# Additions two visits behind in all three edge passes, and the visits' scalars turned in one transposition

## The reference

```
# layer 0, first attention ("gat", 4 heads)
alpha = segment_softmax(leaky_relu(a_src[src] + a_dst[dst]), dst)
x1    = segment_sum(h[src] * alpha, dst)
# layer 0, second attention ("attn", 1 head)
logits2 = (q[dst] * k[src]).sum(-1) * scale
out     = segment_sum(v[src] * segment_softmax(logits2, dst), dst)
# layer 1 ("typed", 8 heads, edge types and edge weights)
a   = exp(alpha - max[dst]);  a = a / denom[dst] * edge_weight
out = segment_sum(x_src[src] * a, dst)
```

## Time and profile before

| | us |
|---|---|
| median of 3 runs | 5183.95 (5179.76 to 5184.89) |
| the profiled execution | 5139.55 |
| its span, first to last instruction | 5137.6 |
| gat: first to last addition | 217.9 to 1597.0 |
| attn: first to last addition | 1838.8 to 3118.0 |
| typed: first to last addition | 3356.8 to 4745.1 |

### The profile page before, as it was taken

How to read it: one execution, slowest core, us unless ns; L and a number is a source line. 1 busy time by engine, 2 the same in 40 slices (tenths; PEclk the granted TensorE clock), 3 DMA queues, 4 the chain that set the end, 5 groups by cost and what they waited for, 6 DMA issues and landing times. The chain is left out here.

```text
span 5137.6 us, 80902 instructions
## 1 busy us (share of the span) xinstructions
PE 3442.0 (67%) x15488; PEld 2347.2 (46%) x15488; DVE 3184.0 (62%) x11098; ACT 1745.4 (34%) x5660; POOL 2637.8 (51%) x2962
## 2 busy tenths in 40 slices
PE   5366666666666556777777778556666666666899
PEld 4244434444444434444444445334443343444898
DVE  6355555555557655665666667655666666667786
ACT  2323323323334534544554555311111111211333
POOL 3555555555540255555555553555555455552787
PEclk8666666666778878888888898766666666767999
DMA  8444444344432433333333334533333333332321
GB/s 131 137 123 116 119 123 118 113 119 124 120 109 69 134 95 102 110 103 101 104 103 100 104 100 143 183 101 102 108 108 105 103 107 107 106 103 63 90 72 54
DMA packets 289304, 556.41 MB, mean 108 GB/s; under 512 B 86392, under 2 KB 183713, under 8 KB 288898
## 3 DMA queue, kind: packets, MB, share of 16 engines
q0 software_dynamic: 115872, 326.30, 23.3%
q10 hardware_dynamic: 97688, 162.20, 10.4%
q1 hardware_dynamic: 75338, 63.47, 4.8%
HBM read 474.96 MB, written 76.78 MB: 107 GB/s over the span
## 5 line engine op out<-in xcount | busy, mean ns | idle before, releaser
L477 PE MATMUL psum<-big,onehots_or_distances 128*128 128x264 f32 (+2 forms) x4992 | 2186.2, 552 | 940.5 <-DVE big L639 309.6
L661 DVE TENSOR_TENSOR acc<-acc,psum 128x264 f32 (+2 forms) x2496 | 1062.4, 426 | 1071.8 <-PE psum L477 347.3
L477 PEld LDWEIGHTS psum<-big,onehots_or_distances 128*128 128x128 f32 x4992 | 1053.0, 256 | 1296.5 <-issue 1018.3
L266 POOL DMA_INDIRECT big<-table_attn,src_by_edge x782 | 739.8, 946 | 785.2 <-SPq L259 374.2
L266 POOL DMA_INDIRECT big<-table_typed,src_by_edge x782 | 740.1, 946 | 669.6 <-SPq L259 441.5
L266 POOL DMA_INDIRECT big<-table_gat,src_by_edge x782 | 739.1, 945 | 662.6 <-SPq L259 438.5
L370 ACT ACTIVATE onehots_or_distances<-psum 128x512 f32<-128x512 f32 x416 | 248.3, 597 | 1786.9 <-PE psum L437 756.5
L639 DVE TENSOR_TENSOR big<-big,psum 128x256 f32<-128x256 f32 x1664 | 670.2, 408 | 63.0 <-issue 33.7
L423 PE MATMUL psum<-big,onehot_t 128*128 x2496 | 485.9, 309 | 192.2 <-issue 117.7
L343 ACT ACTIVATE onehots_or_distances<-iota,tables 128x128 f32<-128x128 f32 x832 | 331.4, 398 | 679.7 <-DVE acc L661 377.0
L504 DVE SCALAR_TENSOR_TENSOR dot_products<-psum,big 128x258 f32<-128x258 f32 x832 | 347.4, 418 | 319.9 <-PE psum L423 150.6
(11 more groups left out here) (280 smaller groups left out, 4420.6 us busy)
## 6 DMA issues: line engine op xcount, KB each, us to landing
onehot_t<-onehots ACTq DMA_DIRECT2D x68, 512.0 KB
big<-visit_positions ACTq DMA_DIRECT2D x52, 512.0 KB
onehots<-big ACTq DMA_DIRECT2D x36, 512.0 KB
big<-onehots ACTq DMA_DIRECT2D x36, 512.0 KB
big<-in_x_dram SPq DMA_DIRECT2D x98, 128.0 KB, 2.5
big<-table_gat,src_by_edge POOLq DMA_INDIRECT x782
big<-table_attn,src_by_edge POOLq DMA_INDIRECT x782
big<-table_typed,src_by_edge POOLq DMA_INDIRECT x782
```

The costliest lines, as they stand in the source:

```text
L266: pool.indirect_dma_start(X[:, t % RING, :], None, ph.table, bass.IndirectOffsetOnAxis(ap=m.src[:, t:t + 1], axis=0)).then_inc(S[f"rows{t ...
L477: nc.tensor.matmul(sum_ps(v), onehot_at(v), rows, start=True, stop=True).then_inc(S["summed"], 1)
L661: nc.vector.tensor_tensor(row, row, sum_ps(v), ALU.add).then_inc(S["added"], 1)
```

## The change

1. In all passes the DVE loop runs one visit longer and calls `add(v - 2)` at `v` where it called `add(v - 1)`. Loading the block numbers and `rescale` move from `v % 16 == 0` to `v % 16 == 1`. Nothing else in a pass moves: scaling, dot products, the parts of the maximum, PE's, ACT's, SP's and POOL's programs and all semaphore values are as before.
2. The per-chunk store of the scalars (7 DMAs, L898) is gone. DVE writes the three numbers of a chunk to columns of one tile; after the last chunk PE transposes that tile once (`turn_scalars`), ACT copies it out of PSUM and SP stores it with one DMA of contiguous rows, then reads it back as before.

```diff
-            for v in range(-3 * G, VISIT_END + 1):
+            for v in range(-3 * G, VISIT_END + 2):
...
-                if 0 <= v < VISIT_END and v % G == 0:
-                    last_blk, blks = (blks[G - 1] if v else None), blocks_of(v // G)
-                if v >= 1:
-                    add(v - 1, last_blk if v % G == 0 and v < VISIT_END else blks[(v - 1) % G])
+                if 0 <= v < VISIT_END and v % G == 1:
+                    last_blk, blks = (blks[G - 1] if v > 1 else None), blocks_of(v // G)
+                if v >= 2:
+                    add(v - 2, last_blk if v % G == 1 and v < VISIT_END else blks[(v - 2) % G])
...
-                if v >= 0 and v % G == 0 and v < VISIT_END:
+                if v >= 0 and v % G == 1 and v < VISIT_END:
                     rescale(v // G, blks[0])
...
+    scalars, scalar_rows = v_.take(3, VC), v_.take(P)[0:3 * VC]
-    scal = [n_.take(3) for _ in range(2)]
...
+    turned_scalars = ps[0:3 * VC, 6, 2 * P:3 * P]
...
-                sp.dma_start(dram.scal[:, c * P:(c + 1) * P].rearrange("a v -> v a"), scal[c % 2], allow_slow_non_contiguous=True).then_inc(S[f"stored{c % 2}"], 16)
...
+            sp.wait_ge(S["scalar_rows"], 1)
+            sp.dma_start(dram.scal.rearrange("a (c p) -> (a c) p", p=P), scalar_rows).then_inc(S["scalars_stored"], 16)
...
+            act.wait_ge(S["scalars_turned"], 1)
+            nc.scalar.activation(scalar_rows, turned_scalars, ACT.Copy).then_inc(S["scalar_rows"], 1)
...
+            def turn_scalars():
+                pe.wait_ge(S["chunk"], VC)
+                pe.wait_ge(S["packed"], VC - 1)
+                pe.wait_ge(S["packed_rest"], VC - 1)
+                nc.tensor.transpose(turned_scalars, scalars.rearrange("p a c -> p (a c)"), m.ident[:, :]).then_inc(S["scalars_turned"], 1)
...
-                nc.vector.tensor_copy(scal[p][:, 0:2], dst_f[:, 0:P:P - 1])
+                nc.vector.tensor_copy(scalars[:, 0:2, c], dst_f[:, 0:P:P - 1])
...
-                nc.vector.tensor_copy(scal[p][:, 2:3], rel[:, 0:1]).then_inc(S["chunk"], 1)
+                nc.vector.tensor_copy(scalars[:, 2, c:c + 1], rel[:, 0:1]).then_inc(S["chunk"], 1)
```

More of the change, by code:

```diff
@@ L908, in _ @@
             sp.dma_start(dram.by_quarter.rearrange("(r p) -> r p", p=P // QUARTER), by_quarter).then_inc(S["places_stored"], 16)
-            sp.wait_ge(S["stored0"], (VC - VC // 2) * 48)
-            sp.wait_ge(S["stored1"], VC // 2 * 48)
+            sp.wait_ge(S["scalar_rows"], 1)
+            sp.dma_start(dram.scal.rearrange("a (c p) -> (a c) p", p=P), scalar_rows).then_inc(S["scalars_stored"], 16)
+            sp.wait_ge(S["stored0"], (VC - VC // 2) * 32)
+            sp.wait_ge(S["stored1"], VC // 2 * 32)
+            sp.wait_ge(S["scalars_stored"], 16)
             sp.dma_start(rows, dram.scal[0:3, :].rearrange("a (k g) -> k a g", g=G)).then_inc(S["rows"], 16)
@@ L1081, in _ @@
                 node(next(step))
+            turn_scalars()
             for i in step:
@@ L1174, in _ @@
                 if c > 1:
-                    dve.wait_ge(S[f"stored{p}"], c // 2 * 48)
+                    dve.wait_ge(S[f"stored{p}"], c // 2 * 32)
                 c_.step(nc.vector.tensor_copy(fields.rearrange("p a e -> p (a e)"), rec[c]))
```

## The result

The changed kernel took 5104.02 us (median of 4 runs, 5094.65 to 5116.35) against 5183.39 (4 runs, 5179.76 to 5184.89): ratio 0.983, 95% interval 0.980 to 0.986. That is 79 us faster where 53 us slower was forecast. Its profiled execution took 5094.65 us, 45 less than that of before. In the table a pass is first to last addition (L661); these lengths are used in all that follows.

What follows compares the result with a forecast made beforehand. It took passes to be bound by waits for late products, paced by (way + lateness) / visits. Terms +122 - 27 - 17 - 10 - 15 = +53 us on the 5183.95 median gave 5237 us, range 5090 to 5325.

Steps and rivals of the forecast that it cites:

- attn's term: attn: additions two behind bring an expansion and a dot into the loop of three banks, +122 us, ends 0 to +266.
- typed's: typed: batch end -17 us, nothing leaves the three-bank way, additions a DVE step later +7; together -10, ends -50 to +60.
- the first stage: Before the passes: one store of the scalars instead of seven saves 15 us, ends -40 to +6.
- What bounds the kernel: All three passes: no engine is full; each visit waits some 0.6 to 0.7 us on something that goes on only beside gathers.
- the lateness: All passes: PE's completions reach other engines late while gathers flow; L = 2.6 us in attn.
- The loop: attn: way from one addition to the next in its bank, three visits, longer by 0.96 us, 0.32 a visit.
- three of its five signs: attn: idle ahead of additions near nothing, ahead of dots up by more than that fall, ACT's idle for additions above 593 us.
- The two signs of its size: attn: additions every 1.7 us or slower beside gathers, above 1.15 us after the last gather.
- The share of idle time: attn: ACT idle for an addition in 593 of 1280 us, 46%, taken as the share of 266 us that counts.
- The first rival: Late products hide attn's longer way (+15), gat -65, typed -25, first stage -20: 5089 us, chance 0.35.
- its first term: gat: one scaling of 0.33 us leaves the four-bank way, 0.08 us a visit, counted at 39%: -27 us.
- The batch's end: gat: the wait for a product moves behind the next batch's first scaling; a third of 50 us, -17.

Runs made afterwards that it cites:

- e7: Kernel before with scalars turned once and no gathers behind the first 44 tiles, additions one visit behind: 3885.35 us against 3993.86.
- e12: Changed kernel with attn's addition ahead of the turn's dot, and block numbers loaded ahead of the maximum's parts in all passes: 4019.25 us against 3991.23 before.
- e3: Changed kernel with a fourth PSUM bank for attn's products, additions two visits behind everywhere: 4013.66 us, 1.0049 of the kernel before.
- e4: Changed kernel with attn's additions back at one visit behind and a fourth PSUM bank for attn: 3983.64 us, 0.9984 of the kernel before.
- e5: The changed kernel itself in a session where products come in time: 4153.70 us, 1.0394 of the kernel before.
- e8: Changed kernel, additions two visits behind, without the gathers behind the first 44 tiles: 4032.83 us, attn 1149.6.
- e17: Additions one behind, DVE held ahead of each ninth addition in attn; maximum's parts and batch's start a visit earlier in gat and typed: 5343.09 us.
- e18: Changed kernel, additions two visits behind, with DVE held by thrown-away additions ahead of each ninth addition in attn: 5515.16 us.
- e11: Additions one behind, PE stopped at each eighth visit, gat's and typed's rows scaled three visits ahead instead of two: 5232.03 us against 5225.77 without the earlier scaling.
- e14: Additions one behind, PE stopped at each eighth visit, maximum's parts and batch's start one visit earlier in gat and typed: 4893.11 us.
- e6: The kernel before, nothing changed, run again for a trace beside the changed kernel: 4005.93 us, where before took 3993.86 in the same session.

## Why the prediction was wrong

Of the 98 us between the forecast's +53 and the traces' -44.9, attn's term makes 74 and typed's 45; gat, the first stage and the rest take 21 back.

**What bounds the kernel** was right in part: waits for products, beside gathers. "The work of a visit is nearly the same in both" stretches was wrong (37 additions with 11 dots), and so 0.6 to 0.7 us a visit "only beside gathers" was too much: without gathers e7 still takes 1.12 to 1.18 us a visit. That "nobody can shorten" the lateness is also right, but the forecast took it for a property of the kernel. The same kernel has passes of 991 us in other sessions.

**attn, the step that failed most.** "I take that share, 0.46 x 266 = +122" was too much by 74 us: the passes show +48.4. The loop is real: the cost goes with the dot (e12) and with the third bank (e3, e4), and three of its five signs came, the wait ahead of additions gone, more than that ahead of dots, and ACT's distances above 593 us. The two signs of its size did not: additions every 1.62 us beside gathers where 1.7 or slower was forecast, and 1.03 behind the last one where it was 1.15. As a price of the loop alone +122 was too small, +158.5 (e5, e8). The share of idle time said how often ACT stood, not how much a longer way would show; in the recorded pair two thirds of the cost disappeared. The first rival had that in words (expansion and dot lie inside the blocks), yet neither PE stopped (+221, +156) nor DVE held (+205) hid it. How the late products of the record do so is open.

**typed, the step whose reasoning was wrong.** "The way holds no scaling before or after, so nothing leaves it", -10 against -55.5. The forecast looked only at the loop of the banks. A blocked addition also holds what stands behind it in DVE's order, and moving it back by a turn lets the maximum's chain and the batch's first scaling pass: -48 with a drifting stop, -133 with a fixed one, -153 with these two moved alone at the fixed one. In the last session, where products are late by themselves, these two alone left typed 30 us longer than the change did (e17 1371.4, e18 1340.9), so there a part of its gain is still unexplained. PE's wait for additions rose above 192 us as forecast, and that did not matter. By the rule of the Trainium skill that the forecast weighed (Perfetto Trace Analysis, Optimization Strategy) an addition moved back without a bank could only cost; for typed the measurement decides against that reading.

**gat**, -31.3 for -44: the size was near, within its ends, but its first term named the wrong cause. A scaling taken from the loop was to give -27, and one more scaling ahead gave nothing at a fixed stop (e11). The batch's end (-17) was a true cause, 76 of e14's 178 us there; the maximum's chain, the other 102, was not seen, and neither was that products would be shorter.

**The first stage**, -9.1 for -15: SP's read came at 117.55 (114 forecast), DVE's wait for PE fell by 10.5 us. e1 has 10 to 14 us for this part alone.

**The median.** A further 34 us of the miss are not in the two traces at all.

**The chances.** What came true is nearest to the first rival's 5089 us, which had 0.35. Its terms for attn (+15), gat (-65) and typed (-25) were each off by some 30 us, so it was near by its total and not by its parts.

## What to carry to other kernels

When an in-order engine meets a wait that comes late and in bursts, list what stands behind it in its order and who waits for that: moving such work ahead of the wait (e14) gained more in all than moving the wait (333 us against 215 at fixed stops), because it cost the third pass nothing; in gat by itself it gained less (178 against 306), and it wasn't run without attn's extra work where products are late. When a wait is moved back past other work, follow each bank's loop through that work; the change was right for two passes and wrong for the one where the moved addition falls behind a dot whose input is queued behind its own product. Compare PE's busy time and granted clock too, and not the waits alone: half of gat's gain at fixed stops was shorter products. Measure a change of order under both conditions: this one is 1.7% faster or 3.9% slower, depending on how late the products come. Where they come in time, the numbers turned once with additions left in place (e1, 3980.89 us) beat both kernels; it was not run where they come late.

## What the runs showed of the hardware

The same kernel took 5184 us in the recorded session, 3991 to 3994 in the next four, and 5195 in the last. The fourth of these (3994) and the last bear the same chip number, 14, so which chip it is doesn't decide it alone. Three groups of e6, the kernel before at 4005.93 us:

```profile
L661 DVE TENSOR_TENSOR acc<-acc,psum 128x264 f32 (+2 forms) x2496 | 1063.0, 426 | 304.7 <-PE psum L477 233.0
...
L266 POOL DMA_INDIRECT big<-table_gat,src_by_edge x782 | 741.4, 948 | 257.7 <-issue 232.7
L639 DVE TENSOR_TENSOR big<-big,psum 128x256 f32<-128x256 f32 x1664 | 672.3, 409 | 72.1 <-ACT psum L335 40.1
```

In the recorded execution the same groups have means of 426, 945 and 408 ns: DVE's and POOL's instructions take equally long. So do the gathers' packets: 29.8% of 4003.9 us and 23.3% of 5137.6 are 1193 and 1197 us of the 16 DMA engines. What differs is idle time, 304.7 us ahead of additions in e6 and 1071.8 then; waits of DVE over 1.5 us are 97, 77 and 103 in the recorded passes and 7, 4 and 3 in e6. PE differs too. The engines in gat, attn and typed of e6, against the earlier trace rows:

```profile
198.00:1190.00 992.00, 747.31 (x3488) 503.66 (x3488) 794.79 (x2833) 424.52 (x1257) 706.19 (x745) 0.81 0.55 159
1395.00:2387.00 992.00, 809.33 (x4282) 531.58 (x4280) 782.25 (x3309) 652.91 (x1810) 711.40 (x750) 0.95 0.47 132
2608.00:3610.00 1002.00, 749.47 (x3488) 490.00 (x3488) 874.12 (x2984) 269.10 (x1159) 706.03 (x745) 0.83 0.51 142
```

The granted clock is 0.81, 0.95 and 0.83 where it was 0.69, 0.86 and 0.69, and PE is busy 2306 us in the three passes where it was busy 2699: 393 of the 1063 us between them. Whether products came late because of the lower clock, or the clock was lower because PE stood still, no run here tells. Gathers flow in both. So "beside gathers" was where the late products showed, and not what makes them by itself. No run here shows their cause.
